# Key projections of a cross attention in tiles of 512, 512, 512 and 72 columns instead of four of 402

## The reference, cut to what matters

```python
q = split_heads(queries @ Wq + bq)      # 16 x 64 x 512, 16 heads of 32
k = split_heads(keys @ Wk + bk)         # keys = values = ctx, 16 x 1601 x 512
v = split_heads(values @ Wv + bv)
scores = jnp.einsum('bhqd,bhkd->bhqk', q, k) / jnp.sqrt(jnp.float32(HD))
scores = jnp.where(mask, jnp.float32(-1000000000000000.0), scores)
attn = jax.nn.softmax(scores, axis=-1)
ctx = jnp.einsum('bhqk,bhkd->bhqd', attn, v)
...
return ctx @ Wo + bo
```

## Time and profile before

| | |
|---|---|
| median of 3 executions | 2826.86 us (2825.01 to 2828.59) |
| the profiled execution | 2828.8 us, its span 2827.0 us |
| mean granted TensorE clock | 0.967 of full speed |
| TensorE busy, matmuls | 2626.3 us (93%), 24440 records |
| TensorE busy, weight loads | 2055.9 us (73%) |
| VectorE busy | 1748.8 us (62%) |
| ScalarE busy | 1450.7 us (51%) |
| GpSimd busy | 113.9 us (4%) |
| the cross attention stage | about 846 to 2250 us |

### The profile page before, as it was taken

How to read it: one execution, slowest core, us unless ns; L and a number is a source line. 1 busy time by engine, 2 the same in 40 slices (tenths; PEclk the granted TensorE clock), 3 DMA queues, 4 the chain that set the end, 5 groups by cost and what they waited for, 6 DMA issues and landing times. The chain is left out here.

```text
span 2827.0 us, 58816 instructions
## 1 busy us (share of the span) xinstructions
PE 2626.3 (93%) x24440; PEld 2055.9 (73%) x24440; DVE 1748.8 (62%) x4188; ACT 1450.7 (51%) x3007; POOL 113.9 (4%) x104
## 2 busy tenths in 40 slices
PE   6999899899959999999999999999999987789987
PEld 3444578679847888887888878888888776667764
DVE  4333542656655666666666676666676688764487
ACT  2111222335535666666666666666666523635774
POOL 0000200120020000000000000000000022010000
PEclk9999999999979999999999999999999988899988
DMA  7999101257751111111111011110111010114300
GB/s 256 304 310 309 56 2 48 94 186 241 243 177 49 50 50 50 33 24 44 50 50 42 21 38 50 49 48 15 38 50 40 31 64 2 40 60 149 124 11 30
DMA packets 202936, 249.41 MB, mean 88 GB/s; under 512 B 77728, under 2 KB 132000, under 8 KB 202416
## 3 DMA queue, kind: packets, MB, share of 16 engines
q1 hardware_dynamic: 193456, 220.49, 24.9%
q10 hardware_dynamic: 6656, 16.78, 1.8%
q0 software_dynamic: 2560, 8.39, 0.8%
HBM read 221.50 MB, written 24.12 MB: 87 GB/s over the span
## 5 line engine op out<-in xcount | busy, mean ns | idle before, releaser
L91 PE MATMUL xa_J<-xa_c_hi,xa_wk_hi 128*128 128x402 f32 x1024 | 359.9, 351 | 1.7 <-POOL xa_m L2516 1.7
L92 PE MATMUL xa_J<-xa_c_lo,xa_wk_hi 128*128 128x402 f32 x1024 | 354.9, 347 | 0.0
L93 PE MATMUL xa_J<-xa_c_hi,xa_wk_lo 128*128 128x402 f32 x1024 | 354.8, 346 | 0.0
L2273 ACT ACTIVATE xa_pr<-xa_pr,xa_ri 128x416 f32<-128x416 f32 x512 | 280.1, 629 | 141.5 <-DVE xa_ri L2401 141.5
L91 PE MATMUL xa_J<-xa_wv_hi,xa_c_hi 128*128 128x512 f32 (+1 forms) x832 | 339.1, 408 | 0.0
L92 PE MATMUL xa_J<-xa_wv_lo,xa_c_hi 128*128 128x512 f32 (+1 forms) x832 | 327.8, 394 | 0.0
L93 PE MATMUL xa_J<-xa_wv_hi,xa_c_lo 128*128 128x512 f32 (+1 forms) x832 | 326.9, 393 | 0.0
L2263 ACT ACTIVATE xa_pr<-xa_pr,xa_local 128x416 f32<-128x416 f32 x512 | 321.6, 632 | 0.0
L2250 ACT ACTIVATE xa_kT<-xa_J,cl_bk 128x402 f32<-128x402 f32 x256 | 151.0, 590 | 328.7 <-PE xa_J L93 323.8
L2375 DVE CUSTOM_DVE_ANT_0 xa_pr<-xa_S,xa_m 128x416 f32<-128x416 f32 x512 | 271.7, 587 | 23.5 <-PE xa_S L2561 22.5
L2413 DVE TENSOR_TENSOR cl_v<-xa_J,main_x 128x512 f32<-128x512 f32 (+1 forms) x208 | 143.4, 689 | 220.6 <-PE xa_J L93 196.7
(11 more groups left out here) (515 smaller groups left out, 5018.0 us busy)
## 6 DMA issues: line engine op xcount, KB each, us to landing
bl_rows<-in_ctx SPq DMA_DIRECT2D x40, 1024.0 KB, 9.0
main_x<-in_ctx_cols SPq DMA_DIRECT2D x192, 201.0 KB, 3.3
bl_cols<-in_ctx_cols SPq DMA_DIRECT2D x24, 1024.0 KB, 10.6
moe_raw<-in_L_ffn_routed_w SPq DMA_DIRECT2D x45, 512.0 KB, 5.0
main_qoT<-in_L_ffn_w ACTq DMA_DIRECT2D x32, 512.0 KB, 3.9
main_x<-in_ctx_cols SPq DMA_DIRECT2D x64, 197.5 KB, 3.3
main_qoT<-in_L_attn_W SPq DMA_DIRECT2D x16, 512.0 KB, 3.6
routed_in<-main_qoT SPq DMA_DIRECT2D x1, 7680.0 KB, 22.5
```

The source lines that it names most:

```text
L91: pe.matmul(out, w_hi, x_hi, start=first, stop=False)
L92: pe.matmul(out, w_hi, x_lo, start=False, stop=False)
L93: return pe.matmul(out, w_lo, x_hi, start=False, stop=last)
L2273: nc.scalar.activation(now, now, ACT.Copy, scale=ri[:, i:i + 1]).then_inc(scaled, 1)
```

## The change

The key tiles are cut at multiples of 512 columns: 0 to 512, 512 to 1024, 1024 to 1536, 1536 to 1608. Loads and splits of the context stay in groups of 402. A tile's chunk now waits for the `c_lo` of the group that holds its last column. At the start of a batch, ScalarE's first two `highs` of group 3 move ahead of `keep_key(w, 0)` and the last two move up to right behind it, ahead of the first exponentials; on VectorE the `lows` of group 3 come after one transposition of the eight instead of three.

```diff
                     act.wait_ge(k_made, 4 * w + j + 1)
-                    nc.scalar.activation(kT[:, j * KG:(j + 1) * KG], J[:, key_place(w, j) % BANKS, 0:KG], ACT.Identity,
+                    k0, k1 = key_columns(j)
+                    nc.scalar.activation(kT[:, k0:k1], J[:, key_place(w, j) % BANKS, 0:k1 - k0], ACT.Identity,
                                          bias=bk_sb[:, g:g + 1]).then_inc(k_stored, 1)
...
                     if b:
+                        highs(b, 3, 0, 2)
                         keep_key(w, 0)
+                        highs(b, 3, 2, 4)
                         exps(w - 1, 0, 2)
                         keep_result(w - 4)
-                        highs(b, 3, 0, 2)
                         keep_key(w, 1)
-                        highs(b, 3, 2, 4)
                         keep_result(w - 3)
...
                     if b:
-                        turn(w - 2, 0, 3)
+                        turn(w - 2, 0, 1)
                         lows(b, 3)
-                        turn(w - 2, 3, 8)
+                        turn(w - 2, 1, 8)
...
                     bank_free(at)
+                    k0, k1 = key_columns(j)
                     for k in range(KC):
                         if g == 0:
-                            pe.wait_ge(c_lo_ready, low_count(b, j, k))
-                        last = product(pe, J[:, at % BANKS, 0:KG], wk_hi[:, k, g * P:(g + 1) * P], wk_lo[:, k, g * P:(g + 1) * P],
-                                       c_hi[:, k, j * KG:(j + 1) * KG], c_lo[:, k, j * KG:(j + 1) * KG], k == 0, k == KC - 1)
+                            pe.wait_ge(c_lo_ready, low_count(b, (k1 - 1) // KG, k))
+                        last = product(pe, J[:, at % BANKS, 0:k1 - k0], wk_hi[:, k, g * P:(g + 1) * P], wk_lo[:, k, g * P:(g + 1) * P],
+                                       c_hi[:, k, k0:k1], c_lo[:, k, k0:k1], k == 0, k == KC - 1)
...
+def key_columns(j):
+    return j * 4 * P, min((j + 1) * 4 * P, KP)
```

## The result

The changed kernel takes 2884.01 us (median of 4 runs, 2882.01 to 2888.78) against 2827.73 us before: ratio 1.0191, 95% interval 1.0179 to 1.0203. It is slower by 56 us. Its profiled execution took 2882.01 us with a span of 2880.2, against 2828.8 and 2827.0, so 53.2 us more on either count.

A forecast was written before the change was run, and what follows sets the result against it. TensorE's product pace was taken to bound the cross attention stage. Each quad goes from 8.803 to 8.352 + 12 x 0.112 = 9.696 us, 0.893 more, x 64 = 57.2; 2826.9 + 57.2 = 2884 us, range 2864 to 2906.

The forecast's parts named there:

- TensorE's pace bounds the stage: Cross attention, 846 to 2250 us: a microsecond of product pace is a microsecond of the run; other engines cost nearly nothing.
- Small products are paced by their load, 0.112 us: Last key tile of each quad: 12 products of 72 columns at 0.112 us each, near ends 0.110 and 0.118.
- The bound from below: Load of 72 columns lasts 141 ns against 189 for 128: 0.86 ns a column, so 128 need at least 0.110 us.
- Wide key products cost what value products cost, 0.232: Each quad's 36 key products of 512 columns take 0.232 us each, 8.352 us together.
- The last store's cover: ScalarE's 72-column store before scores: the value tile behind the last key tile covers it by 2.0 us without a result between.
- the prediction's 1363: Sum in us of the stage's key products 563, value products 579, scores 119 and results 102, of 1404.
- The batch edge: Third key tile needs group 3 whole; moved splits ready some 2.5 us early, price 0; otherwise 0.5 to 1 us at 15 edges.
- The first batch: As the stage opens, the first tile waits for lows of group 1: some 0.5 us once, left out of the sum.
- (a): Rival: small products' pace follows their columns down to 72, load hidden, 0.036 us each; 2826 us; chance 5%.
- (b): Rival: loads overlap two deep, small products paced at 0.094 us; 43 us more, 2870 us; chance 4%.
- (c): Rival: small reduced products lose their speed, 0.224 or 0.189 us each; 2970 or 2943 us; chance 7% together.
- (d): Rival: the clock falls once in each quad around the small tile, adding 117 us, near 3000 us; chance 2%.

## Why the prediction was right

The range, the direction and the mechanism held. That the median is 2884 to the microsecond is in part luck: one term was 3 us too large, and the medians happened to lie 3 us further apart than the profiled executions.

*TensorE's pace bounds the stage.* Shown: every edit of its products moved the stage by its own arithmetic (+86.4 for 86, +31.1 for 30, -63.4 for 64), and edits of ScalarE's and VectorE's order moved nothing.

*Small products are paced by their load, 0.112 us.* Right: 0.1115 in the trace, the same for 8, 72 and 144 columns, and 0.058 for half an operand. The bound from below was weaker than it was stated: with the 142 ns of the row shown in the earlier trace rows it is 0.107 us and not 0.110. By the load rule in the section LDWEIGHTS of "TensorE: Matmul & The Clock Gate" in the Trainium skill (columns over 1.2 GHz, 107 ns for 128) the sum was 53 us. The traces show 4 to 5 ns more for a load, and the 53.2 us of the profile don't make the rule better, because of the next term.

*Wide key products cost what value products cost, 0.232.* The mis-sized term: 0.2306. It takes 0.0014 x 36 x 64 = 3.2 us off 57.2. With 0.1115 in place of 0.112 another 0.4 goes, and the sum is 53.6, against 52.7 for the stage and 53.2 for the span. The medians lie 56.3 us apart, those of the new tiles alone 53.1. The runs of one kernel spread over 6 to 7 us in the result and over up to 17 in the experiments, so the 3 us between are within what this measurement can tell.

*The last store's cover.* Forecast 2.0 us without a result between. In the changed kernel the 72-column store stands at 1334.13 for 0.30 us, not the 0.21 I took, and the value tile ends near 1336.1: cover 1.7 us. TensorE's loads wait for ScalarE's store 0.5 us in the whole stage. Right, but not the whole of the covers: the other chain, from the exponentials over VectorE's sums to the masks, has no cover left in two quads of a batch, where the second burst takes 1.33 us and not 0.98. The change moved nothing there (the sums wait behind the store of a value tile, which TensorE paces), but "nearly nothing that ScalarE or VectorE does here costs anything" was too much said. If all batches are like this one, the stalls come to 0.35 x 2 x 16 = 11 us, an estimate (the profile puts down 8.3 us in 36 waits). They would be part of the 41 us between the prediction's 1363 and the stage's 1404, which it left without a term; since they stand on both sides, the forecast of the difference lost nothing by it.

*The batch edge.* The third tile starts at 1310.20 and VectorE ends lows of group 3 at 1307.22:

```profile
1305.26 1.96 DVE L106 TENSOR_TENSOR xa_c_lo<-main_x,xa_c_hi 128x395 fp32r<-128x395 f32 x4
...
1310.20 0.50 PE L91 MATMUL xa_J<-xa_c_hi,xa_wk_hi 128*128 128x512 f32 x1
```

Three us early where 2.5 were forecast, so price 0 is right. What I had read into the reorder, that the tile would otherwise be held, was more than it is: the kernel without it loses nothing.

*The first batch.* Forecast some 0.5 us. The first key product's idle went from 1.70 to 2.30 us, 0.6. It lies ahead of the stage as I count it: 52.7 + 0.6 is the 53.2 of the span within a tenth. What I had not seen is the clock. Behind that wait it fell to the lower level in the first tile:

```profile
847.07 0.47 PE L91 MATMUL xa_J<-xa_c_hi,xa_wk_hi 128*128 128x512 f32 x1 [2.30 <-DVE xa_c_lo L106]
...
848.26 0.63 PE L92 MATMUL xa_J<-xa_c_lo,xa_wk_hi 128*128 128x512 f32 x1
848.69 0.63 PE L93 MATMUL xa_J<-xa_c_hi,xa_wk_lo 128*128 128x512 f32 x1
```

Products of 512 columns are 0.43 us apart there. The level is back at 851 us, and there is a second fall at about 872 to 875, behind the first scores. The kernel before has one fall, at about 867 to 873. Over 846 to 880 us the mean clock is 0.90 in both, so the sum keeps its balance. All seven kernels profiled here whose first key product waits 2.3 us have a fall in their first tile, and none of the four in which it waits 1.7 us has one.

*The rivals.* (a), the pace of the columns, fell with twelve products of 8 columns. (b), two loads deep, fell with the interleaved tiles and with the 0.111. The 81 ns that the same page of the Trainium skill gives in its section Back-to-back issue gap is shown in no run here, at 8, 72, 128 or 144 columns. (c), slow narrow reduced products, fell with 240 columns at 0.1125. (d), a clock that falls in each quad, didn't come: 1.00 from 900 us to the end of the stage.

## What to carry to other kernels

Where each product brings its own 128-column load, each product costs the larger of its own columns' time and 0.111 us, at the upper clock and for the reduced type of this kernel; the two meet at some 240 columns. A wide neighbour does not pay for a small product: taken in turn, they cost the same. Cut a length that isn't a multiple of 512 into equal pieces, or keep the remainder above that width: four of 402, or 456, 456, 456 and 240, cost the same within what these runs can tell, and 512, 512, 512 and 72 costs 0.84 us a quad for no instruction fewer. To price a width that a trace doesn't have, look for the pace of weight loads beside the smallest products that the trace does have, and don't extend a line through widths that all lie above the crossing.

## What was not expected of the hardware

- The first small product starts 0.23 us behind a wide one, and the next starts 0.03 us behind it; the bill comes one product late and ends in the tile behind (0.47 us for the value tile's first product, 0.39 otherwise). A mean over a form's records (0.26 to 0.28 us for 72 columns) shows none of it.
- Only one load is made ahead, even where the product ahead is 0.23 us long and a load needs 0.111: a pair of 512 and 72 columns takes 0.343 us.
- Key products of 512 columns go at 0.2306 us and value products at 0.232, both with 128x128 loads. Why was not tried.
- A 72-column store out of PSUM on ScalarE takes 0.304 us, a 64-column one elsewhere 0.208.
- Where the clock falls in the first 35 us of the stage differs between kernels: twice in the changed one (848 to 851 and 872 to 875), once before (867 to 873), and not at all with the new order alone, whose stage is 2.4 us shorter. The fall in the first tile goes with the longer first wait; what decides the one behind the first scores stays open.
